# Three weight-block units behind each query block, in place of nine at the head of each head group

## What is computed

```python
xn = _layernorm(x)
q, k, v = (split_heads(xn @ W + b) for W, b in ((Wq, bq), (Wk, bk), (Wv, bv)))
att = softmax(where(causal, q @ k.T / 8, -inf))
s = layernorm((att @ v) @ Wo + bo) * gamma + beta
h = silu(xn @ (w_gate / 127).T) * (xn @ (w_up / 127).T)
g = silu(h @ (w_down / 127).T)
return x + s * g
```

## Time and profile before

| what | value |
|---|---|
| timed runs | 7100.77 and 7304.64 us, median 7202.71 |
| profiled execution | 7105.78 us; span of its slowest core, core 1, 7104.2 us |
| spans of the eight cores | 7044.4 to 7104.2 us, granted clock 0.895 to 0.900 |
| PE busy with matmuls | 5708.8 us, 80% of the span |
| ACT busy, DVE busy | 1695.8 us (24%), 1368.1 us (19%) |
| attention of b = 0, first to last projection start | 326.2 to 2235.1 us |
| attention of b = 1, first to last projection start | 3969.3 to 5494.3 us |

### The profile page before, as it was taken

One profiled execution on the slowest core, in us unless ns is written; L12 is line 12 of the kernel. 1 busy time (PEld: TensorE's weight loads), 2 busy tenths in 40 slices (PEclk: granted clock), 3 DMA queues, 4 the chain that ended last, 5 costly groups with the idle time before them and its releaser, 6 DMA issues.

```text
span 7104.2 us, 79725 instructions; the slowest of 8 cores (7044.4 to 7104.2 us)
## 1 busy us (share of the span) xinstructions
PE 5708.8 (80%) x30072; PEld 2859.4 (40%) x30072; DVE 1368.1 (19%) x2326; ACT 1695.8 (24%) x3084; POOL 55.2 (1%) x108
## 2 busy tenths in 40 slices
PE   1296696686786885899995799899999985999998
PEld 1132232232232234677663333233333333766765
DVE  3212012022012014121122211121110114112111
ACT  4131231331321311111112333323333311111111
POOL 0000000000000000000000000000000000000000
PEclk9997797787888897999997798888998987999999
DMA  5502102102111133666665200000000032667666
GB/s 172 152 14 39 32 14 37 30 17 35 27 21 27 30 95 89 151 158 153 148 164 151 52 11 10 14 15 13 14 12 9 5 97 65 151 147 165 154 148 146
DMA packets 1512815, 529.73 MB, mean 75 GB/s; under 512 B 1384182, under 2 KB 1474550, under 8 KB 1512444
## 3 DMA queue, kind: packets, MB, share of 16 engines
q1 hardware_dynamic: 1390332, 419.75, 25.3%
q10 hardware_dynamic: 107136, 69.22, 3.2%
q0 software_dynamic: 14976, 35.66, 3.1%
HBM read 474.19 MB, written 69.21 MB: 76 GB/s over the span
## 4 chain that ended last, share of the span: by engine, by line
PE 73%; DMA 13%; DVE 5%; ACT 4%; issue 4%; SPq 1%; ACTq 0%; DVEq 0%; POOLq 0%
PE pb L781 15%; PE pb L556 10%; PE pb L1040 9%; PE pb L1028 9%; PE pb L734 8%; DMA pool_b<-scr_wblk 6%; PE pb L1104 5%; PE pb L608 5%; PE pb L908 5%; DMA scr_wblk<-pool_b 4%; PE pb L673 2%; PE pb L743 1%; DMA pool_f<-x 1%; PE pbt L310 1%; ACT pool_f L807 1%
## 5 line engine op out<-in xcount | busy, mean ns | idle before, releaser
L781 PE MATMUL pb<-pool_f 128*65 128x512 f32 (+3 forms) x2560 | 1152.1, 580 | 0.0
L758 ACT ACTIVATE pool_f<-pb,tiny 128x512 f32<-128x512 f32 (+3 forms) x1280 | 757.8, 623 | 1458.4 <-PE pb L743 1013.2
L1028 PE MATMUL pb<-arena_a,pool_b 128*128 128x256 bf16 x6144 | 740.9, 274 | 179.2 <-DMA pool_b<-scr_wblk 179.0
L1104 PE MATMUL pb<-pool_b 128*128 128x512 bf16 x3072 | 695.9, 383 | 109.2 <-DMA pool_b<-scr_wblk 108.2
L1040 PE MATMUL pb<-arena_a,pool_b 128*128 128x256 bf16 x6144 | 735.7, 273 | 9.7 <-ACT pool_f L1117 9.2
L556 PE MATMUL pb<-arena_a,pool_b 128*128 128x512 bf16 x3072 | 713.4, 391 | 11.3 <-DMA pool_b<-scr_whilo 11.3
L1028 PEld LDWEIGHTS pb<-arena_a,pool_b 128*128 128x128 bf16 x6144 | 602.8, 98 | 260.2 <-issue 187.4
L734 PE MATMUL pb<-pool_b 64*128 64x512 bf16 (+3 forms) x3840 | 693.1, 380 | 0.2 <-ACT pool_f L758 0.2
L1040 PEld LDWEIGHTS pb<-arena_a,pool_b 128*128 128x128 bf16 x6144 | 601.3, 98 | 84.2 <-issue 12.8
L781 PEld LDWEIGHTS pb<-pool_f 128*65 128x65 f32 x2560 | 325.6, 148 | 515.1 <-issue 495.1
L310 PE MATMUL pbt<-idb_s,pool_b 128*128 128x128 bf16 x576 | 72.1, 304 | 532.5 <-DMA scr_wblk<-pool_b 391.8
(11 more groups left out here) (82 smaller groups left out, 2742.4 us busy)
## 6 DMA issues: line engine op xcount, KB each, us to landing
pool_b<-scr_wblk SPq DMA_DIRECT2D x1152, 256.0 KB, 3.5
pool_f<-x SPq DMA_DIRECT2D x96, 512.0 KB, 4.4
pool_b<-scr_o SPq DMA_DIRECT2D x64, 512.0 KB, 5.5
pool_b<-scr_whilo SPq DMA_DIRECT2D x96, 256.0 KB, 4.0
scr_wblk<-pool_b ACTq DMA_DIRECT2D x72, 256.0 KB, 5.0
scr_whilo<-pool_b ACTq DMA_DIRECT2D x64, 256.0 KB, 3.1
scr_o<-pool_b ACTq DMA_DIRECT2D x128, 128.0 KB, 1.7
y<-pool_f ACTq DMA_DIRECT2D x32, 512.0 KB, 3.7
```

The lines of the kernel that those rows point to most:

```text
L758: e.activation(d, s_, AF.Exp, bias=bc)),
L781: e.matmul(o, l, r, start=st, stop=sp)),
L1028: e.matmul(o, l, r, start=st, stop=sp)),
L1104: e.matmul(o, l, r, start=st, stop=sp)),
```

## The change

The call at the head of each head group of b = 0 goes; in its place, three units are issued at the end of each query block of b = 0, between the last emit_av and the Ln of the softmax sums. Nothing else differs. The 72 units are used up after 24 query blocks, that is, in head groups 0 to 5.

```diff
         for hg in range(8):
-            if b == 0:
-                emit_wblk_units(9)
             rd_prev = {}
...
                     prev = sc
                 emit_av(prev)
+                if b == 0:
+                    emit_wblk_units(3)
                 rcs = {}
```

## The result

In the executions compared, the changed kernel takes 0.9926 of the time of before, with a 95% interval of 0.9902 to 0.995: 0.7% less, a gain clear of the noise but within the 2% that count as no change. The fastest executions are 7040.35 us against 7095.79, 55 us apart.

The account below looks back on a forecast made before the run. PE, working in order, was held by 391.8 us of waits for weight-block stores. Removed 473.4, added 301 + 106 + 13.5 = 420.5, net -53 from the profiled 7105.8: 7053 us, range 6990 to 7150.

Parts of the forecast that it names:

- waits for a store: PE at line 310, before the weight-block transposes: 48 waits in place of 64, 294 us in place of 392.
- start of the phase: Head of the phase, without a bunch: PE waits 13.5 us for the six weight slices of head group 0.
- a slot, to the next scores: Three units after a query block's last AV matmul: two steps of 7.15 plus 1.03, 15.33 us on PE.
- Ln behind the last transpose: ACT after the three units: Ln starts 1.27 us after the last transpose, behind copy and store issue.
- a head group with four slots: Head groups 0 to 5, with units after each query block: near 282 us each (215 to 218 and 67).
- clock behind a slot, against before: Dense work after each three units: half-speed spell no worse than today's, taken as 0 between -3.15 and +3.15 us.
- The bunches: Eight groups of nine units removed from PE's path: 66.7 + 7 x 58.1 = 473.4 us.
- ACT's chain: Query block's end: stores issued ahead of Ln and Exp delay ACT, and so PE's second broadcast, 1.4 us each time.
- The clock paying a whole further spell of 3.15 us per slot: Dense work behind each of 24 slots: one more half-clock spell, 76 us slower, 7129 us; chance 0.15.
- The clock coming back early: Behind the slots: full speed when dense work starts, today's fall gone, 57 us faster, 6996 us; chance 0.14.
- The hidden stores: Inside the slots: the 48 store waits vanish, 294 us less, 6759 us; chance 0.01.
- Longer steps: Inside the slots: each step always 8.7 us, 74 us on top, 7127 us; chance 0.05.

Follow-up runs that it names:

- the filler run: The changed kernel plus twelve matmuls of unread product behind the first and second unit of each of the 24 slots; 0.9918 of the kernel before.
- the spread version: Against the changed kernel, one unit behind the AV product of every fourth key tile of b = 0 instead of three per query block; 0.939 of the kernel before.
- 71 waits: Against the changed kernel, all 72 units in one bunch at the head of the phase; 1.0064 of the kernel before.

## Why the prediction was right or wrong

**The level was wrong.** The text put the changed kernel at 7053 us and its range from 6990 to 7150, and the median of its executions, 7365 us, lies far outside. The step that failed is the sentence of the sum that "the sum goes by the profiled one": it took the level of one execution at 7105.8 us, although the two timed runs beside it already lay 2.8% apart and their median 97 us higher. What the runs showed in its place: the kernel before, unchanged, had a median of 7304 us in the same comparison, 198 above that level, and the twelve executions of the changed kernel go from 7040 to 7813, with two of them, 7040 and 7053, at the forecast. A range for an absolute time has to hold that spread; mine held only the mechanisms of the change. No step of the change explains the 7365, and what makes one execution of a kernel longer than another was not tested by any run.

**The difference was right, to the last digit by luck.** Forecast was 7053 / 7105.8 = 0.9926, -53 us; measured are a ratio of 0.9926 and 55 us between the fastest executions. The steps, on core 1:

| step | forecast | measured |
|---|---|---|
| waits for a store | 48, 294 us | 48, 278.9 us |
| start of the phase | 13.5 us | 14.4 us |
| a slot, to the next scores | 15.33 us | 13.9 to 14.8 us, mean 14.3 |
| Ln behind the last transpose | 1.27 us | 1.35 us |
| a head group with four slots | 282 us | 278 to 280 us |
| clock behind a slot, against before | no change | 0.73 against 0.75 over 12 us |

The slot was the term that was sized too high, by some 1.0 us, 24 us in all. The wait in a slot is 5.8 us instead of the 6.1 of a bunch, and the first transposes run at the full clock (0.61 us instead of 1.03), which the forecast, taking them from a bunch, had overlooked. Two small terms go the other way. The bunches were taken at 58.1 us each, and on cores 0 to 3 of the kernel before the eight, the first with its start, sum to 462 to 472 us instead of 473.4; and the clock behind a slot costs 0.3 us more than before (0.73 against 0.75 over 12 us). From the first slice load to the start of head group 7 core 1 gained 70 us instead of 53 (1905.7 against 1975.4); cores 0, 2 and 3 gained 52, 51 and 67. Core against core the gain differs by as much as the term was off, and that the total came out at 55 and the ratio at the forecast 0.9926 is in part luck.

**ACT's chain** as a term of 1.4 us per slot was right: the stretches between slots, which hold the clock's part too, grew by 0.9 to 1.8 us on core 1 over those of before (28.8 against 27.9 us, 39.9 against 38.4, 50.4 against 48.6), and taking the stores out from ahead of the Ln gave back 1.5 us at such a boundary.

**The rivals.** The clock paying a whole further spell of 3.15 us per slot, given 0.15, falls by the filler run and by the windows: the boundary's own fall is there with and without the filler, and grew by 0.3 us. The page "TensorE: Matmul & The Clock Gate" of the Trainium skill, section "HAM oscillation — how this bites in real kernels", says that a wait in every round makes PE pay the fall of the clock in every round. The trace agrees, with a fall behind every slot, but the old boundary fell too (0.75 against 0.73), so that 24 slots cost next to nothing more. The clock coming back early falls by the windows: 0.60 over the first 7 us of dense work, not 1.00. Even the filler, which had PE at full speed at the slot's end, did not keep it up through ACT's chain. The hidden stores, given 0.01, did not come with this change, and the spread version shows why: the same 72 units, with work between them, cost next to nothing, 0.939. Longer steps did not appear: the longest wait in the slots of core 1 was 6.3 us.

**Why so little.** Eight bunches of nine became 24 slots of three. That takes 16 waits of 64 away and 52 us off the start, and puts 24 times 1.4 us and more on ACT's chain in their place. The position in the attention was never what cost; it was the lack of work between two units that share one staging tile.

## What to carry to other kernels

An engine that works in order hides a transfer only behind the instructions that stand between its issue and its wait: moving a block of work elsewhere keeps its inner waits, and counting these (groups, times the units in one less one) together with the start of the phase forecast this kernel's ratio to a few tenths of a per cent at 48, 64 and 71 waits. Spread single units with more work between them than a transfer takes, or double the buffer that they share; and where another engine issues their stores, issue them behind the short operations of that engine that the next stretch waits for, not ahead of them. Forecast the ratio and the absolute time apart, and let the range of the second hold the spread that the timed runs already show.

## What the runs showed of the hardware

Ten units of transposes in a head group, 6 us of PE's time, lengthened it by 0.6 us on the average of 48 groups: in two groups of like length PE was busy for 199.6 us with them and without, at a granted clock of 0.91 and 0.89. With twenty units the clock paid back little or nothing. Filler matmuls that kept PE busy through the stalls raised the mean granted clock from 0.90 to 0.92 and shortened the phase by 13 us of 2132. A store of 256 KB that has a second one beside it landed after 5.5 to 5.6 us (median) instead of 4.8, and was waited for 6.2 us on average, 7.6 at the most.
